# First attention of a fused two-layer kernel: units of two heads by 256 queries, row maxima spread by transposes, chunks of queries taken from the last to the first

## What is computed

```python
H, QL, KL, DN, DR, DV = 16, 192, 64, 128, 64, 128
q = (rmsnorm(x @ w_q_a) @ w_q_b).reshape(b, s, H, DN + DR)
ckv = x @ w_kv_a
kv = (rmsnorm(ckv[..., :KL]) @ w_kv_b).reshape(b, s, H, DN + DV)
qf = concat(q_nope, rope(q_pe)); kf = concat(k_nope, rope(k_pe))
scores = einsum('bqhd,bkhd->bhqk', qf, kf) / sqrt(DN + DR)
p = softmax(where(causal, scores, lowest))
return einsum('bhqk,bkhd->bqhd', p, v).reshape(b, s, H * DV) @ w_out
```

## Time and profile before

| what | value |
|---|---|
| time, median of 3 runs | 2014.09 us (2013.54 to 2016.42) |
| the profiled execution's own time | 2015.19 us |
| its span, first to last instruction | 2013.2 us |
| first attention's heads in it (L1217 to the last L1303) | 141.3 to 1267.7 us |
| PE busy | 1776.6 us, 88% |
| DVE busy | 1515.9 us, 75% |
| ACT busy | 1271.1 us, 63% |
| POOL busy | 1003.5 us, 50% |

### The profile page before, as it was taken

The page is one execution under the profiler, slowest core; times in us unless marked ns, Lnnn a source line. Parts: engine busy times, 40 slices in busy tenths (PEclk is TensorE's granted clock), DMA queues, the critical chain, the costliest instruction groups (busy, mean ns, idle before and its releaser), DMA issues. The chain is left out here.

```text
span 2013.2 us, 28359 instructions
## 1 busy us (share of the span) xinstructions
PE 1776.6 (88%) x9496; PEld 1022.7 (51%) x9496; DVE 1515.9 (75%) x2366; ACT 1271.1 (63%) x2491; POOL 1003.5 (50%) x892
## 2 busy tenths in 40 slices
PE   4668999999999999999999997565979899999996
PEld 3546655555556555555565553455644344444445
DVE  6765888778888778878878886677565888888716
ACT  1147887788888787778877875111334377777760
POOL 0005989788888888788888987002401000000110
PEclk8788999999999999999999998677976699999998
DMA  3200000000000000000000000111330200110001
GB/s 97 76 9 15 1 1 15 1 1 14 1 1 15 1 6 9 1 14 1 1 6 1 1 1 0 45 45 37 74 74 1 32 1 1 19 16 2 2 1 42
DMA packets 26704, 34.40 MB, mean 17 GB/s; under 512 B 5312, under 2 KB 19648, under 8 KB 26432
## 3 DMA queue, kind: packets, MB, share of 16 engines
q1 hardware_dynamic: 25360, 31.28, 6.6%
q10 hardware_dynamic: 1200, 1.31, 0.2%
HBM read 26.03 MB, written 6.29 MB: 16 GB/s over the span
## 5 line engine op out<-in xcount | busy, mean ns | idle before, releaser
L1192 POOL TENSOR_TENSOR lath_summed<-lath_summed,lath_held 128x512 f32<-128x512 f32 (+3 forms) x528 | 595.7, 1128 | 46.5 <-ACT lath_held L1095 6.6
L1903 ACT ACTIVATE atth_probs<-atth_score 128x512 f32<-128x512 f32 (+3 forms) x640 | 293.4, 542 | 166.7 <-PE atth_score L1822 164.7
L1262 DVE TENSOR_TENSOR lath_held<-lath_held,lath_shift 128x512 f32<-128x512 f32 (+1 forms) x448 | 339.3, 791 | 26.2 <-PE lath_shift L1010 24.8
L1090 ACT ACTIVATE lath_held<-lath_score 128x512 f32<-128x512 f32 (+1 forms) x448 | 293.1, 686 | 83.1 <-issue 31.7
L1862 DVE TENSOR_REDUCE atth_maxima<-atth_slot 128x2 f32<-128x1024 f32 (+3 forms) x288 | 286.4, 1042 | 61.6 <-PE atth_slot L1805 60.6
L1095 ACT ACTIVATE lath_held<-lath_held 128x512 f32<-128x512 f32 (+1 forms) x448 | 303.6, 720 | 27.4 <-DVE lath_held L1262 24.5
L998 PE MATMUL lath_out<-lath_held,lat_latent 128*64 128x512 f32 (+3 forms) x1280 | 312.7, 553 | 6.4 <-ACT lath_held L1095 5.6
L983 PE MATMUL lath_score<-lath_query_hi,lat_key_hi 128*128 128x512 f32 (+3 forms) x640 | 261.8, 409 | 23.0 <-ACT lath_held L1090 21.2
L1750 POOL TENSOR_SCALAR_AFFINE_SELECT atth_probs<-atth_probs 128x512 f32<-128x512 f32 x64 | 40.6, 635 | 445.0 <-ACT atth_probs L1903 445.0
L987 PE MATMUL lath_score<-lath_query_hi,lat_key_lo 128*128 128x512 f32 (+3 forms) x640 | 255.9, 400 | 0.0
L1215 DVE TENSOR_TENSOR lath_largest<-lath_score,lath_largest 128x256 f32<-128x256 f32 (+3 forms) x336 | 221.9, 684 | 22.5 <-PE lath_score L987 20.3
(11 more groups left out here) (346 smaller groups left out, 2973.1 us busy)
## 6 DMA issues: line engine op xcount, KB each, us to landing
att_first_query<-att_scratch SPq DMA_DIRECT2D x12, 256.0 KB, 9.3
atth_query<-att_scratch SPq DMA_DIRECT2D x12, 256.0 KB, 9.1
ffn_a_w<-in_L_ffn_W SPq DMA_DIRECT2D x2, 1024.0 KB
lat_raw_out<-in_L_attn_w_out SPq DMA_DIRECT2D x8, 256.0 KB, 2.7
lat_rope<-in_c_rope_feature SPq DMA_DIRECT2D x1, 2048.0 KB, 10.4
ffn_b_w<-in_L_ffn_W SPq DMA_DIRECT2D x2, 1024.0 KB, 7.1
mix_a_factors<-in_L_ffn_factors SPq DMA_DIRECT2D x8, 256.0 KB, 4.3
att_scratch<-attp_high SPq DMA_DIRECT2D x4, 512.0 KB, 3.2
```

Of the source, the lines that this page charges most:

```text
L1090: nc.scalar.activation(slot(n)[:, tiles, q0:CH], score_bank[n % 2][:, tiles, q0:CH], ACT.Copy)\
L1192: nc.gpsimd.tensor_tensor(total[:, q0:CH], so_far, slot(n)[:, i, q0:CH], ALU.add).then_inc(s["tiles_summed"], 1)
L1262: nc.vector.tensor_tensor(slot(n)[:, tiles, q0:CH], slot(n)[:, tiles, q0:CH], shift[:, q0:CH].unsqueeze(1).broadcast_to([P, count, CH - q0 ...
L1903: nc.scalar.activation(probs[:, step % PROB_STEPS, h, q0:CH], score_bank[u % 3][:, q0:CH], ACT.Exp, scale=SCALE1)\
```

## The change

- A unit is both heads of a pair and 256 queries. A step is two key tiles by 2 x 256 queries, so it is as wide as before; a unit of block j (0 to 7) has j + 1 steps, 288 in all. Only the last step is diagonal, in two parts: 512 columns, and 2 x 128 for the second tile. The helpers `part_columns` and `by_head` take the columns of both heads.
- The chunks of 512 queries come in the order 3, 2, 1, 0, two blocks in each.
- The maxima are no longer negated and laid out by ACT. PE transposes the column `row_max`, read 128 times over with a step of zero (new L1027), four times a unit, and DVE subtracts instead of adding. `ones_r`, `minus_ident` and `shift_diag` go.
- The running maximum uses three buffers of 512 in place of four; a unit of block 1 takes its maximum of two SBUF tiles. The fold is two instructions of 64x256, one for each head.
- The column sums of a chunk are copied into `out_t` (new L1120), which the projection of the chunk before still reads, so that copy waits for the projection.
- `query_hi` and `query_lo` have two slots, each for both heads of a chunk. A unit's scores wait for both heads' low parts. The high part of a chunk's query waits for the scores of the chunk two before it.
- The second pass is due 11 steps after the first, and the planner's durations are new.

```diff
-LATENT_UNITS = [(pair, j, h) for pair in range(PAIRS) for j in range(NCH) for h in range(2)]
-LATENT_STEPS = [(u, s) for u, (_, j, _) in enumerate(LATENT_UNITS) for s in range(key_tiles(j) // 2)]
+UNIT = CH // 2
+LATENT_CHUNKS = (3, 2, 1, 0)
+LATENT_UNITS = [(pair, 2 * c + e) for pair in range(PAIRS) for c in LATENT_CHUNKS for e in range(2)]
+LATENT_STEPS = [(u, s) for u, (_, j) in enumerate(LATENT_UNITS) for s in range(j + 1)]
-SECOND_PASS_AFTER = 12.0
-QUERY_SLOTS = 3
+SECOND_PASS_AFTER = 11.0
+QUERY_SLOTS = 2
...
+    u, s = LATENT_STEPS[g]
+    return [(slice(0, 2), 0)] if s < LATENT_UNITS[u][1] else [(slice(0, 1), 0), (slice(1, 2), P)]
+def part_columns(tensor, tiles, q0):
+    if q0 == 0:
+        return tensor[:, tiles, :]
+    return tensor[:, tiles, :].rearrange("p t (h q) -> p (t h) q", h=2)[:, :, q0:UNIT]
+def by_head(row, q0):
+    return row.rearrange("p (h q) -> p h q", h=2)[:, :, q0:UNIT]
...
+        due = FIRST_STEP[2 * k] - 7.0 + n % 2
+        free = ("scores", FIRST_STEP[2 * (k - QUERY_SLOTS + 1)] - 1) if k >= QUERY_SLOTS else None
...
-        add("scalar", 1.2, urgent, ("diag", u), ("turn_max_out", u), of("spread", u - 1))
-        add("tensor", 0.35, urgent, ("spread", u), ("diag", u), of("add", FIRST_STEP[u] - 1))
+        add("tensor", 0.55, urgent, ("spread", u), ("turn_max_out", u), of("add", FIRST_STEP[u] - 1))
...
-            add("scalar", 0.55, urgent, ("sums_out", k), ("sums", k), of("turn_sums", k - 1))
+            add("tensor", 1.1, urgent, ("sums", k), ("sum", FIRST_STEP[u] - 1), ("sum", last), of("project", k - 1, 1))
+            add("scalar", 0.6, urgent, ("sums_out", k), ("sums", k))
...
-                            pe.wait_ge(s["query_lo_done"], u + 1)
+                            pe.wait_ge(s["query_lo_done"], 2 * (u // 2) + 2)
...
-                        pe.wait_ge(s["diag_ready"], TPC * (n + 1))
+                        pe.wait_ge(freed(("turn_max", n)), use["turn_max", n] // 2 + 1)
...
-                        nc.tensor.matmul(shift[:], ones_r[:], shift_diag[:].rearrange("p t q -> p (t q)"), start=True, stop=True)\
-                          .then_inc(s["spread_done"], 1)
+                        for i in range(TPC):
+                            last = nc.tensor.transpose(shift[:, i * P:(i + 1) * P], row_max[:, n % 2, i:i + 1].broadcast_to([P, P]), core.ident)
+                        last.then_inc(s["spread_done"], 1)
...
-                        for i in range(TPC):
-                            nc.scalar.activation(shift_diag[:, i], minus_ident[:], ACT.Copy, scale=row_max[:, n % 2, i:i + 1]).then_inc(s["diag_ready"], 1)
...
-                            wait_side(act, ("turn_sums", n - 1))
-                        nc.scalar.activation(sums_t[:], side(("sums", n))[:], ACT.Copy).then_inc(freed(("sums", n)), 1)
+                            wait_side(act, ("project", n - 1, 1))
+                        nc.scalar.activation(out_t[:], side(("sums", n))[:], ACT.Copy).then_inc(freed(("sums", n)), 1)
...
-                        if n >= QUERY_SLOTS:
-                            act.wait_ge(s["scores_done"], FIRST_STEP[n - QUERY_SLOTS + 1])
+                        k = n // 2
+                        if k >= QUERY_SLOTS:
+                            act.wait_ge(s["scores_done"], FIRST_STEP[2 * (k - QUERY_SLOTS + 1)])
```

228 lines of the change are left out of this document (113 added, 115 removed).

## The result

The changed kernel takes 1959.41 us (median of 4 runs, 1956.53 to 1962.4), the kernel before in the same measurement 2015.08 us (4 runs, 2013.54 to 2016.42). The ratio is 0.9733, 95% interval 0.971 to 0.9756: 55.7 us or 2.7% faster, where 1968 us was forecast. The profiled execution took 1960.14 us, with a span of 1958.3.

The account below looks back on a forecast made before the run. No engine was saturated; four in-order lists of about equal length wait for each other. From 2015.2 us: -28.5 POOL work, -23 wait between passes, +8 start, -7 and +4 end, giving 1968.7, so 1968 us; range 1932 to 2014.

Parts of the forecast that it names:

- The work: Pieces and one operation saved in the stage: POOL 28.5 us less, taken as the gain; ACT 117.1, DVE 21.4 less.
- eight more and eight fewer cancel: POOL's sums: eight more of two held tiles and eight fewer from zero, taken to cancel.
- PE: PE's work in the stage: +14 us for transposes against fewer score products; unchanged, give or take 15 us.
- The wait between the passes: Chain from a unit's maxima to its second pass: shorter without ACT's layout, -23 us, ends 0 and -60.
- The waits before a unit's first sum: Sign in the changed kernel's profile: POOL's waits there should total 50 to 70 us, not 88.
- The start: Stage's first scores: they wait for both heads' low parts, +8 us, from 0 to +16.
- The end: Behind the last spread: shorter last unit, 22.7 us becoming 16, so -7; new chain for chunk 0, +4.
- The wait of the last chunk's sums for the projection of chunk 1: Stage's end: chunk 0's sums are copied into the tile chunk 1 is projected from; +4 us, up to 11.
- The late query: Rival at each new pair: second head's query comes too late; 6.6 us at 7 boundaries cancels the gain; chance 0.10.
- PE sets the pace: Rival for the stage: PE's 96% is near the truth, so work and wait give nothing; 2020 us, chance 0.09.
- ACT held the rest: Rival for the stage: with ACT's load down, PE's 45.3 us of waits vanish too; 1923 us, chance 0.17.
- The clock: Rival for PE: 192 more matmuls of the transposing kind lower the granted clock, costing 10 us; 1978 us, chance 0.04.

Follow-up runs that it names:

- a_pool_less: Changed kernel with POOL leaving out the second of two sums in 168 full steps after a unit's first: 1939.23 us.
- b_both: Kernel before with the spread by four transposes and chunks in the order 3, 2, 1, 0, units still of one head and 512 queries: 1987.41 us.
- b_chunks: Kernel before with only the chunks turned round to the order 3, 2, 1, 0: 1980.79 us.
- a_diag: Changed kernel with the layout by ACT and the one spreading product put back in place of the transposes: 1979.01 us.
- b_transposes: Kernel before with only the spread of the row maxima by four transposes, without ACT's layout: 1988.76 us.
- a_chunks: Changed kernel with chunks in the order 0, 1, 2, 3: 2004.37 us.
- a_after12: Changed kernel with the second pass planned 12 steps after the first in place of 11: 1957.35 us.
- a_due9: Changed kernel with a chunk's two low query parts planned 9 steps ahead of its first scores in place of 7: 1960.31 us.
- a_act_load: Changed kernel with four ACT copies of 128x128, for which nothing waits, behind each unit's last copy of scores: 1972.86 us.
- a_sums_t: Changed kernel with the separate tile for turned sums back, so a chunk's sums no longer wait for the projection before: 1967.01 us.
- b_both11: Kernel before with transposes, chunks in the order 3, 2, 1, 0, and the second pass planned 11 steps after in place of 12: 1977.41 us.

## Why the prediction was right, and where its terms were not

The forecast was 1968 us, the time 1959: right in sign and within the range, but several terms were off and made up for each other. The middle was to gain 28.5 + 23 = 51.5 us and gained 42.0; the end was to gain 7 - 4 = 3 us and gained 17.3. That the total came out within 9 us is in part luck.

**The work.** Wrong by size for the engine that was taken, and wrong in taking it: with 232 us less on POOL the middle is only 25 us shorter (a_pool_less). POOL's sums were to fall by 28.5 us. Added up over the stage, they fell from 674.6 us (336 x 1.321, 64 each of 0.511, 0.776 and 1.088, 48 x 1.287 and 16 x 1.069 in the groups of before) to 663.7, by 10.9. Of the difference 11.4 is that 392 sums now take 1.350 us each. Another 5.6 lie in "eight more and eight fewer cancel": 1.7 in unequal prices, 1.287 for a first sum against 1.069 from zero, and the rest in that both grew, to 1.335 and 1.210. What made them grow is in the last section. DVE's instructions fell by 12.0 us in all (949.7 to 937.7), but its busy time rose from 887.2 to 889.8: neighbours overlap by some 0.08 us each, 62.5 us before and 47.9 now, so a removed piece gives back less than its bar. ACT's fell by 136 us and its busy time by 87, for the same reason. The forecast for it, 117 us, lay between.

**PE** was priced at nothing, "give or take 15 us". That is the step that was furthest off. Its busy time in the middle fell by 35.7 us, and its idle time by 6.4: together the 42.0 by which the middle is shorter. POOL's work fell by 7 us there and its idle time by 35, from 170.4 to 135.5. The b_both kernel and the changed one differ in the form of the unit and what came with it (the delay of 11, the query slots). PE's score and values groups in b_both, 150 to 1275 us:

```profile
L998 PE MATMUL lath_out<-lath_held,lat_latent 128*64 128x512 f32 (+3 forms) x1280 | 313.2, 553 | 8.9 <-DVE lath_out_whole L1280 8.2 <-ACT lath_held L1096 0.5
L983 PE MATMUL lath_score<-lath_query_hi,lat_key_hi 128*128 128x512 f32 (+3 forms) x640 | 261.2, 408 | 17.9 <-ACT lath_held L1091 17.9
L987 PE MATMUL lath_score<-lath_query_hi,lat_key_lo 128*128 128x512 f32 (+3 forms) x640 | 252.8, 395 | 0.0
```

and in the changed kernel:

```profile
L1014 PE MATMUL lath_out<-lath_held,lat_latent 128*64 128x512 f32 (+1 forms) x1152 | 302.9, 589 | 5.0 <-DVE lath_out_whole L1303 4.3 <-ACT lath_held L1114 0.7
L998 PE MATMUL lath_score<-lath_query_hi,lat_key_hi 128*128 128x512 f32 x576 | 247.9, 430 | 24.3 <-ACT lath_held L1108 17.8 <-POOL lath_query_lo L1224 6.2
L1003 PE MATMUL lath_score<-lath_query_hi,lat_key_lo 128*128 128x512 f32 x576 | 231.6, 402 | 0.0
```

A tenth of the instructions is gone on the same columns, and half of the mask products (58.9 to 36.3 us), and PE's busy time in the middle fell with them: 1019.8 to 986.7 us, and the middle from 1057.3 to 1030.0. The prediction priced the 192 score products fewer at half of 20 us and left out the values products.

But PE's work is not the time either. From b_chunks to a_diag, the same step without the transposes, PE lost 27 us of work and gained as much idle time: 1047.0 and 1045.9 us. The middle is PE's work plus what PE waits, and the table shows which part touches which: the transposes take 21 to 23 us of PE's idle time alone on the kernel before (49.7 to 29.1) and last on the new one (65.8 to 43.3), but only 2 between b_chunks and b_both. The form of the unit takes 17 to 33 us of PE's work in all three pairs, and gives 29, 26 and 6 us of idle time back (b_transposes to a_chunks, b_chunks to a_diag, b_both to the changed kernel): only where both other parts are there is it a gain. The falling order takes 10 us of idle time and 15 of work on the units of before, 14 and 10 on the new ones. On the units of before with the transposes (b_transposes to b_both) it does the opposite: 8 us of idle time and 7 of work more.

The work adds up once the clock is taken out. With 0.47 us taken off for each us at the lower level, an estimate, PE's work in the middle is 1005.7 us before, 1013.2 in b_transposes, 1004.2 in b_chunks, 1012.7 in b_both, 980.0 in a_chunks, 970.2 in a_diag and 981.4 in the changed kernel. Then the form of the unit takes 31 to 34 us in all three pairs, the transposes cost 7 to 11 where 14 were forecast, and the order of the chunks is worth 2 us at most either way: what it did to PE's busy time was the clock. The idle time does not add up. It depends on the whole order as it is written out: a_after12 and a_due9 moved the middle by 9 and 7 us without touching any instruction's cost.

**The wait between the passes** was forecast at -23 us; b_transposes shows -25, and a_diag 14 to 23. The mechanism was right as far as first sums wait less in both pairs, though part of the gain was ACT's load, which cost 6.6 us in a_act_load and which the prediction had counted under work and held to be free. It also left out that PE's idling at chunk 2 lets the clock fall. The waits before a unit's first sum were to be 50 to 70 us and are 38.4; here the order of the chunks helped (62.1 us in a_chunks, to 1240 us).

**The start** was +8 and is +6.9, or +7.65 from the first low part, in both profiles of the changed kernel. PE waited 5.00 us there for the second low part.

**The end** was -7 and +4, and is -17.3. The last two units are short, and behind the last spread POOL had only their sums left: 7.4 us, not 16. (It was 22.5 us before; the 22.7 of the prediction run to the start of PE's next product.) The wait of the last chunk's sums for the projection of chunk 1, +4, was not there: that projection ends at 1206.6 us, and the product over the last sums starts at 1207.45. a_sums_t agrees.

**The rivals.** The late query was there as a gate: at 5 of 7 new pairs the first scores start within 0.2 us of the second head's low part. At the fifth pair, PE's timeline shows:

```profile
678.19 0.50 PE L998 MATMUL lath_score<-lath_query_hi,lat_key_hi 128*128 128x512 f32 x1 [0.91 <-POOL lath_query_lo L1224]
```

But from 200 us on such waits come to 5.3 us of weight loads and 1.2 of products, and a_due9 gained nothing that can be told. The second pass covers them, as the prediction held. PE sets the pace was given 0.09 and its form, no gain at all, was wrong; its premise, that the 96% are near the truth, was nearer than I granted: with 232 us taken from POOL the middle falls by 25 us and stops with PE 98% busy. That PE bounds it there is the likeliest reading of that row; no kernel made PE's work less alone, so it isn't shown. ACT held the rest at most in part (a_act_load). The clock was better, not worse, with 192 transposes more: 11.3 us at the lower level for 35.6, and none at all in b_transposes. The Trainium skill, TensorE: Matmul & The Clock Gate, "Part 4: PE-mode transpose", whose rule that transposes don't count as busy in the same way spoke for that rival, isn't contradicted; the rows only show that these few do no harm between matmuls.

What stays open: why b_both comes out no better than either part. Its waits of the first sums are as long as b_transposes' (64.5 and 63.3 us), though they come once a pair. Its middle is 15 us longer: 8 us of PE's idle time, and 7 of its work, for which 15.2 us at the lower clock against none are enough. The earlier second pass of b_both11 gives 8.5 us back. Why the falling order gains 25 us without the transposes and loses 15 with them, no run says.

## What to carry to other kernels

Where several in-order engines feed each other, part the time of the stage into the work and the idle time of its fullest engine, and price every edit on both; the sum of instruction bars of an engine that isn't full (POOL here: 232 us removed, 25 gained) says little. In a two-pass pipeline whose second pass may start on a unit only when the first has ended it, growing units can starve the second pass and short units last make the end short. Shrinking units were worth 24 us of middle and 18 of end in the changed kernel, 25 and 16 in the kernel before. But in the kernel before with transposes the middle got 15 us longer, so only the end is safe to count on. Look at the granted clock where the fullest engine idles: here 35.6 us at half the clock hid in a mean of 0.98, and made equal work look like 15 us more. Price pieces from start to start and not by their bars, and after a change in a written-out order expect some 7 to 10 us either way from the order itself.

## What the runs showed of the hardware

The transposes with a zero-step operand take 279 ns, as whole tiles do, and follow each other at (0.65 - 0.28) / 3 = 0.12 us.

The granted clock fell to 1.2 GHz after stretches in which PE idled (busy 1.94 of 4 us), and products of 512 columns then started 0.43 us apart in place of 0.23.

POOL's sums of 128x512 grew from 1.321 to 1.350 us, and its first sums from 1.287 to 1.335, although they do the same on the same tiles; with 168 of them left out (a_pool_less) they take 1.321 again, its first sums, though, 1.369:

```profile
L1210 POOL TENSOR_TENSOR lath_summed<-lath_summed,lath_held 128x512 f32<-128x512 f32 x224 | 296.0, 1321 | 80.9 <-ACT lath_held L1114 72.2
```

The maximum of two SBUF tiles on DVE grew too, from 1.118 to 1.131 us. The means hide two kinds of instruction. Sums that overlap no DVE instruction with two SBUF inputs (these maxima, the sines, the splits of the weights) take 1.285 us before (247 of 336) and 1.287 in the changed kernel (264 of 392), none over 1.31. Those that overlap one take 1.418 (89) and 1.481 (128), up to 1.84. On DVE's side the maximum takes 0.69 us where POOL happens to be idle, once in each of the two profiles. One meeting in the changed kernel:

```profile
952.56 1.28 POOL L1218 TENSOR_TENSOR lath_query<-lath_turn_a,lath_turn_b 128x512 f32<-128x512 f32 x1
952.72 1.68 DVE L1232 TENSOR_TENSOR lath_largest<-lath_largest 128x512 f32<-128x512 f32 x1
953.80 1.73 POOL L1208 TENSOR_TENSOR lath_summed<-lath_summed,lath_held 128x512 f32<-128x512 f32 x1
```

The Trainium skill, SBUF — State Buffer, "Who interferes with whom", says that a DVE instruction with two SBUF inputs and a GpSimd one that reads SBUF contend. The traces agree: the growth lies in the sums that overlap such an instruction, and there are more of those. No run took the DVE instructions away.
